# Taking xs, gate and turned-y tiles out of their PSUM bank one step later, in a selective-scan kernel

## What is computed

```python
def _ssm(h, in_w, xproj_w, dt_bias, A_log, Dskip, out_w):
    xz = h @ in_w
    xs, z = jnp.split(xz, 2, axis=-1)
    xs = jax.nn.silu(xs)
    proj = xs @ xproj_w
    dt = jax.nn.softplus(proj[..., :D_INNER] + dt_bias)
    Bm = proj[..., D_INNER:D_INNER + D_STATE]
    Cm = proj[..., D_INNER + D_STATE:]
    A = -jnp.exp(A_log)
    def step(hst, ins):
        dt_t, B_t, C_t, x_t = ins
        dA = jnp.exp(dt_t[:, :, None] * A)
        hst = hst * dA + (dt_t * x_t)[:, :, None] * B_t[:, None, :]
        y_t = jnp.einsum('bds,bs->bd', hst, C_t)
        return (hst, y_t)
    ...
    y = jnp.swapaxes(ys, 0, 1) + xs * Dskip
    return y * jax.nn.silu(z) @ out_w
```

## Time and profile before

| | |
|---|---|
| median of three runs | 3474.05 us (3472.1 to 3475.24) |
| the profiled execution, its own time | 3473.82 us |
| its span in the profile | 3472.0 us |
| the scan, from the first L1525 to the last L1534 | 65.5 to 2651.3 us |
| busy in the whole span | PE 96%, DVE 86%, ACT 84%, POOL 66% |
| mean granted TensorE clock | 0.98 |

### The profile page before, as it was taken

How to read it: one execution, slowest core, us unless ns; L and a number is a source line. 1 busy time by engine, 2 the same in 40 slices (tenths; PEclk the granted TensorE clock), 3 DMA queues, 4 the chain that set the end, 5 groups by cost and what they waited for, 6 DMA issues and landing times.

```text
span 3472.0 us, 59905 instructions
## 1 busy us (share of the span) xinstructions
PE 3320.5 (96%) x22946; PEld 2561.0 (74%) x22946; DVE 2981.9 (86%) x2916; ACT 2902.2 (84%) x4709; POOL 2305.9 (66%) x1087
## 2 busy tenths in 40 slices
PE   8999999999999999999999999999899989999999
PEld 5888988898898888988988898898786432222344
DVE  4988999999999999999999999999996688888231
ACT  6999999999999999999999999999994437777620
POOL 1878998898898889988988988899685000000000
PEclk8999999999999999999999999999999989999999
DMA  3223222222222222222222222222211241220000
GB/s 114 74 71 79 80 68 71 64 69 69 69 85 69 68 65 74 69 71 63 76 69 70 63 69 68 65 69 69 78 61 34 55 110 19 37 31 7 0 7 19
DMA packets 193185, 214.21 MB, mean 62 GB/s; under 512 B 75617, under 2 KB 144993, under 8 KB 192641
## 3 DMA queue, kind: packets, MB, share of 16 engines
q1 hardware_dynamic: 192898, 210.36, 21.2%
HBM read 192.19 MB, written 18.06 MB: 61 GB/s over the span
## 4 chain that ended last, share of the span: by engine, by line
PE 73%; ACT 12%; DVE 7%; POOL 3%; issue 3%; DMA 1%; SPq 0%; DVEq 0%; ACTq 0%; POOLq 0%
PE psum L1534 19%; PE psum L1309 18%; PE psum L1528 14%; PE psum L1525 11%; ACT arena L967 5%; ACT arena L950 4%; DVE arena L1215 3%; PE psum L1621 3%; PE psum L1610 3%; POOL arena L725 3%; PE psum L1585 2%; DVE row_max L1262 2%; PE psum L1554 1%; POOL arena L709 1%; DVE skip_w L1288 1%
## 5 line engine op out<-in xcount | busy, mean ns | idle before, releaser
L725 POOL TENSOR_TENSOR arena<-arena 128x1024 f32<-128x1024 f32 x1024 | 2236.6, 2193 | 377.4 <-DVE arena L1215 355.2
L1215 DVE TENSOR_TENSOR_SCAN arena<-arena,psum 128x512 f32<-128x512 f32 x2048 | 2377.4, 1230 | 118.6 <-PE psum L1528 76.2
L967 ACT ACTIVATE arena<-arena,a_neg 128x512 f32<-128x512 f32 x2048 | 1421.0, 713 | 48.7 <-PE psum L1528 48.2
L1534 PE MATMUL psum<-ident,arena 128*128 128x128 f32 x8192 | 1241.7, 275 | 8.0 <-POOL arena L725 7.9
L950 ACT ACTIVATE arena<-arena,bT 128x512 f32<-128x512 f32 x1536 | 1095.8, 714 | 0.0
L1528 PE MATMUL psum<-ident,arena 128*128 128x128 f32 x6144 | 1016.3, 275 | 0.0
L1534 PEld LDWEIGHTS psum<-ident,arena 128*128 128x128 f32 x8192 | 968.4, 142 | 14.1 <-POOL arena L725 12.9
L1525 PE MATMUL psum<-arena 128*128 128x128 f32 x4096 | 838.7, 287 | 75.2 <-DVE arena L1215 62.3
L1525 PEld LDWEIGHTS psum<-arena 128*128 128x128 f32 x4096 | 652.1, 192 | 307.7 <-issue 177.1
L1528 PEld LDWEIGHTS psum<-ident,arena 128*128 128x128 f32 x6144 | 749.9, 143 | 0.0
L1309 PE MATMUL psum<-arena 128*128 128x512 f32 x1472 | 705.3, 601 | 11.6 <-issue 5.1
(11 more groups left out here) (120 smaller groups left out, 1097.0 us busy)
## 6 DMA issues: line engine op xcount, KB each, us to landing
arena<-bc_dram SPq DMA_DIRECT2D x256, 512.0 KB, 3.7
arena<-diag_dram SPq DMA_DIRECT2D x224, 128.0 KB, 2.1
arena<-qk_dram SPq DMA_DIRECT2D x96, 128.0 KB
diag_dram<-arena SPq DMA_DIRECT2D x32, 256.0 KB, 4.5
qk_dram<-arena SPq DMA_DIRECT2D x12, 512.0 KB, 4.9
arena<-in_x SPq DMA_DIRECT2D x4, 512.0 KB, 10.5
arena<-in_up_w SPq DMA_DIRECT2D x1, 2048.0 KB, 11.2
out_xT<-arena SPq DMA_DIRECT2D x8, 256.0 KB, 2.3
```

What stands on the lines that cost most here:

```text
L725: pool.tensor_tensor(out[:, :, way], h_now[:, :, way], c_row, ALU.mult)\
L967: act.activation(decay[:, w % AHEAD, f], dt_[:, u % 2, f], ACT.Exp, scale=a_neg[:, d, f, st:st + 1])\
L1215: dve.tensor_tensor_scan(hs[:, w % RING, f, rows][:, way], decay[:, w % AHEAD, f, way], psum[:, 4 + n % U_BANKS, way], end_state(w - DS, f ...
L1534: return pe.matmul(psum[:, c, f * P:(f + 1) * P], hs[:, w % RING, f, at:at + P], ident[:, :], is_transpose=True, start=False, stop=w % DS ...
```

## The change

ACT reads xs, zs and yT tiles out behind the step two after the one in which PE made them, instead of one after. dt tiles were read out two steps after theirs before and still are. Everything else of `act_turns` (abs and exp of dt, square, std, silu, softplus, bT, dtxT, the even up tiles) and the DVE's `recip scale` keep their steps; only the way in which they are written changes. PE's order, its banks and the DMA queue's order are as before.

```diff
-EVICT = 1
+EVICT = {"dt": 2, "xs": 2, "zs": 2, "yT": 2}
...
-            step, long_ = TURN[u].get(st - EVICT), TURN[u].get(st - EVICT - 1)
-            todo = [long_] if long_ and PIECES.get(long_[0]) else []
-            todo += [step] if step and not PIECES.get(step[0]) else []
-            if step and step[0] == "sum":
-                todo.append(("std",) + step[1:])
+            todo = []
+            for back in (2, 1):
+                step = TURN[u].get(st - back)
+                if step and EVICT.get(step[0], 1) == back:
+                    todo.append(step)
+                    if step[0] == "sum":
+                        todo.append(("std",) + step[1:])
...
-            for k, kind in ((2, "abs"), (3, "exp")):
-                back = TURN[u].get(st - EVICT - k)
+            for k, kind in ((3, "abs"), (4, "exp")):
+                back = TURN[u].get(st - k)
...
-            back = TURN[u].get(st - EVICT - 1)
+            back = TURN[u].get(st - 2)
             if back and back[0] == "sum":
                 todo += steps("recip scale", *back[1:])
```

## The result

| | before | after |
|---|---|---|
| median of six runs each | 3472.58 us (3470.84 to 3475.24) | 3457.45 us (3456.27 to 3459.33) |
| span of the profiled execution | 3472.0 us | 3454.8 us |
| ratio, with its 95% interval | | 0.9956 (0.9943 to 0.9969) |

The change makes the kernel 15.1 us faster; the interval is 11 to 20 us. 13.3 us were forecast. After the change all lines behind the edit stand two further down: L818 is L820, L967 is L969, L1215 is L1217, L1525 is L1527.

A forecast was written before the change was run, and what follows sets the result against it. PE bounds steps 11 to 33, but behind the Silu block ACT's late place holds PE in seven units. 7 x 1.9 = 13.3 us less gives 3460.5 us; forecast range 3455 to 3467 (0.76).

The forecast's parts named there:

- The waits that go, and where they go to: Scan: ACT's xs/zs read-out waits (52.5 us) go to near 0; second-decay waits (48.2 us) grow by 20 to 40 us.
- ACT's place at step 33: Unit 3: second decay 2.40 us earlier, less 0.50 us for a moved read-out, so the Silu block comes 1.9 us earlier.
- What it is worth: Behind the Silu block, units 1 to 6: PE's step 35 comes 1.9 us earlier, 11.4 us in all; DVE late next.
- rival C: More gain: DVE's queueing and lower-clock stretches behind the stalls go too, up to 1.5 us more a unit, 3450 to 3455; 0.10.
- Unit 0: Last xs read-out's 4.40 us wait goes; ACT 2.40 us earlier less 0.50 us, so 1.9 us gained.
- Nothing is given back: Behind the Silu block everything, the softplus stall behind step 50 too, only moves earlier; 1.9 us neither given back nor added to.
- yT and the bank: Scan: moved yT read-outs cost ACT 0.50 us each as before, under cover; PE's possible bank wait taken as 0.
- The last unit and behind the scan: Last unit gains nothing, since its Silu block doesn't hold PE; it and all behind the scan stay as now.
- Rival A: No effect: PE doesn't wait for ACT's place behind the Silu block, or DVE or POOL returns the time; 3468 to 3477; 0.08.
- B: Slower: PE waits 0.4 us a side tile for the bank if ACT's lead stays 3.25 us; 38 us, 3512; 0.06.

The follow-up runs named there:

- the copies: Kernel before and changed kernel, each with both Silu of the block made plain copies: 3458.6 us and 3456.22 us, kernel before 3471.12 us.
- yT_only: Kernel before with only the yT tiles read out one step later: 3473.09 us, before 3471.68, ratio 1.0004.
- zs_only: Kernel before with only the zs tiles read out one step later: 3461.58 us, before 3471.68, ratio 0.997.
- last_zs: Kernel before with only the last of the four zs tiles of units 1 to 6 read out one step later: 3465.53 us, before 3471.68, ratio 0.9982.
- copy_before: Kernel before with both Silu of the block made plain copies, without the two table loads: 3458.6 us, before 3471.12, ratio 0.9963.
- xs3: Changed kernel with xs and yT tiles read out three steps behind theirs: 3628.0 us, kernel before 3472.09, ratio 1.0447.

## Why the prediction held, point by point

- **The waits that go, and where they go to.** Right. L820 waits nowhere; the other limit took 32 us of the 52.5 us, inside the 20 to 40 forecast.
- **ACT's place at step 33.** Right to hundredths. By the limit I put the block 1.9 us earlier against PE; it came 1.93 us earlier in unit 3. DVE's wait behind the block is 0.1 to 0.5 us in units 1 to 6, as forecast. In unit 0, where 1.9 us were forecast, ACT's step 34 starts 3.32 us behind PE's instead of 5.24, so 1.92.
- **What it is worth.** Right for units 1 to 6: step 34 shrinks by 1.88, 1.91, 1.93, 1.91, 1.90 and 1.91 us, in sum 11.4 as forecast. One point was luck: I named DVE as next in line, but the copies show that PE's own work is the floor, 5.86 us in the odd units and 5.67 in the even ones. Units 1 and 5 sit on that floor now, unit 3 is 0.09 us above it and the even ones 0.4 us. In units 1 and 5 PE waits for nothing in step 34 any more, so the 1.9 us that ACT gained only just fitted. A larger gain at ACT would have been cut off there, which rival C didn't see.
- **Unit 0.** The term was 1.9 us and step 34 shrank by 3.04. The rest is the clock: before, a stretch at the lower level lay over this step. With a shorter such stretch, in `yT_only`, where ACT's place is the old one (5.24 us behind), the step took 10.04 us, with none and the new place 8.07. The prediction had given up to 2.2 us for this possibility and not counted it. It goes with the change: in the four kernels with Silu in which ACT begins step 34 5.24 us behind PE (`before`, `yT_only`, `zs_only`, `last_zs`) the granted clock over this step is 0.80, 0.92, 0.79 and 0.79, in the six in which it begins 3.3 to 3.6 us behind it is 1.00 each time.
- **Nothing is given back.** Right for units 1 to 6: steps 35 to 50 unchanged, the softplus stall unchanged (steps 50 to 53 of units 1, 3 and 5 take 17.40 us before and after). Not in unit 0: there ACT is late again at the softplus block, and steps 50 to 53 take 20.39 us, not 19.42 (step 51 alone 10.01 us, not 8.70). Part of what the clock gave in steps 34 and 35 goes back in this way. From step 34 to step 54 unit 0 is 3.15 us shorter than before (107.65 against 110.80), and 1.95 us shorter than in `yT_only` (109.60), whose unit 0 is the same program as before.
- **yT and the bank.** Right: yT alone changes nothing, and PE never waits for a read-out ahead of a side tile.
- **The last unit and behind the scan.** The stage behind was the same to 0.04 us. The last unit was to stay as it is and took 2.4 us more in this profile. In `copy_before`, in which no read-out is moved, it took 346.7 us as well. The windows over the whole unit give a granted clock of 0.98 before and 0.97 in the other two, and 1.6 us of the 2.4 lie in its steps 0 to 3 (18.90 against 20.55). So such a length needs no moved read-out, and the clock makes most of it.
- **Rival A** falls by the steps 34 and by the copies; **B** exists but isn't met by this change; **C**'s lower-clock stretch behind the block went in unit 0; in units 1 to 6 there was none before either.

The total came to 15.1 us, and to 12.9 when measured again; 13.3 were forecast, 11.4 us in units 1 to 6 and 1.9 us in unit 0. About 2 us are left of the first measurement and nothing of the second. In the profiles such differences fall to the clock; whether any of it belongs to the change, beyond unit 0's stretch, isn't shown. The interval of 11 to 20 us holds both 15.1 and 13.3.

## What to carry to other kernels

An in-order engine that reads a tile out as soon as it is made waits for the maker each time, and each wait resets its lead; if a long block without output for the others comes later, that lost lead is paid for there, so look at the lead at the block and not at the sum of the waits. Such waits must be taken away as a row, up to the last one ahead of the block: in units 1 to 6 the longest ones alone (xs, 25.6 of 52.5 us of waits) gave nothing, the last one alone 0.5 us a unit, the four zs together (15.8 us of waits) all of it. How late a read-out may be is set by the moment at which the maker asks for the buffer again, and the step past that point costs far more than the waits did.

## What the runs showed of the hardware

**The lower clock comes with short pauses too, but not each time.** In `xs3` a PE pause of 2.04 us was followed by a piece of twice the length (1.96 us against 1.02) and a granted clock of 0.82 over the step. The Silu stall of unit 3 before, with a pause of 1.75 us, had none there. In all kernels steps 0 to 3 of the even units 2, 4 and 6 took either 18.66 or 20.3 us with the same work in them, according to whether a stretch at 1.2 GHz fell there. The changed kernel took 18.66 us at all three places in both of its profiles, so the pattern may not be all chance. Steps 11 to 34 of units 1 to 6, in contrast, are the same to 0.02 us in every kernel but `xs3`. So at this level one profile's difference of two spans isn't the effect: 17.2 us in the spans, 14.5 us in the steps that the change touches.

**A table load costs what its row shows.** Block with loads: 6.43 us; without them 3.6 us. The difference of 2.8 us is two loads of 1.28 us and 0.1 us around each, for the two activations are as long with Silu (1.91 and 1.90 us) as with a copy (1.89 and 1.90). The Trainium skill (ScalarE: Activation LUTs, section "What ACT_TABLE_LOAD costs") gives about 1283 ns for the load, as in these rows, and 1380 ns more for a drain, 2.66 us for each switch. The second part isn't seen here: it would make 5.3 us for the two switches, and 2.8 us were measured, 1.4 us each.
